# A selective-scan and mixture-of-experts layer: a third group of states multiplied by c on VectorE from PSUM

## The chip, the cores and the metric

The kernel runs on one core of a Trainium2 chip. The metric is the device time of one execution in microseconds (us); the median of several runs counts. The engines are TensorE (PE in the profile, its weight loads PEld), VectorE (DVE), ScalarE (ACT), GpSimd (POOL) and SyncE (SP, here only a queue for transfers).

## The reference

x holds 32 sequences of 256 steps and 128 features, fp32. Each sequence goes through a selective scan with residual, and then through a feed-forward network with 8 routed experts (the 2 best are used) and shared ones. Cut to what matters:

```python
u, o = split(layernorm(x) @ W_in.T)                  # 256 channels each
u = silu(conv4(u) + conv_b)
g = u @ W_gate.T                                     # 64 delta_lo, 16 b, 16 c
delta = softplus(g[..., :64] @ W_delta.T + delta_bias)
def step(h, inp):                                    # h: 256 channels x 16 states
    d_t, u_t, b_t, c_t = inp
    h = exp(A * d_t[..., None]) * h + (d_t * u_t)[..., None] * b_t[:, None, :]
    return h, einsum('nhs,ns->nh', h, c_t)           # y_t
y = (scan(step) + D * u) * sigmoid(o) * o
x = x + y @ W_out.T
x = x + ffn(layernorm(x))    # sum over experts of combine * (silu(x wg) * (x wu)) wd, + the shared one
```

## The kernel before

The program is a software pipeline written out by hand. Each engine has one list of instructions, in order; semaphores tie them together, and nothing reorders them later. Step k of the loop works on several sequences at once: layernorm, convolution and projections of sequences k+2 and k+3, delta of k+1, the scans of k, the output projection and router of k-1, and the feed-forward part of f = k-2.

The 256 channels x 16 states of a sequence are cut into 8 groups q = 0 to 7 of 128 partitions x 4 blocks x 256 steps (groups 0 to 3 are channel half 0, 4 to 7 half 1). For each group:

- ScalarE writes the decays exp(A d) into decay_ps, a PSUM tile with two halves; group q uses half q % 2 (decays, L489).
- GpSimd makes inject = (d u) b (inject_group, L410). dd holds d and d u, and SyncE spreads it to the tile rep by 8 transfers a sequence.
- VectorE scans (scan, L687). The result goes to the SBUF tile state, or, for the groups in OWN, back over its decays in decay_ps.
- The states are multiplied by c: GpSimd does it from state into read (read_group, L420), or, for the groups in OWN, VectorE from decay_ps into the single tile read_own (read_own_group, L699), and then it clears the first column of that half with a memset (L701).
- TensorE sums the products over the states into y_ps (sum_states, L894), which take_y (L722) multiplies by the gate.

Before a half of decay_ps is written again its last group must have been scanned, or, for a group of OWN, multiplied:

```python
if (q - 2) % GROUPS in OWN:
    act.wait_ge(decay_zero, owned_before(at - 1) + 1)
else:
    act.wait_ge(state_done, count(at - 1))
```

The feed-forward part has 7 pairs of chunks: gates (L902) and ups (L911) on TensorE, silu (L476) on ScalarE, gated_up (L708, called by pairs) on VectorE. Spread_comb (L923) spreads the combine weights over partitions, weigh (L716) multiplies by them, and down (L936) adds the 14 chunks into down_ps. Three PSUM banks, work0 to work2, are shared by all of this, by the table COMB_BANK and its like, so that many of these wait for one another. Softplus (L553) writes delta, which L790 on VectorE multiplies by u into dd; x1 (L781) is the sum of the projection and x; L804 and L809 are mean and variance of x_in, L816 and L827 those of x1.

Of the kernel before, what the change touches and what calls it, by code (L numbers as in the profile page):

```python
# [12 lines left out]
P = 128  # L13
# [32 lines left out]
OWN = (0, 4)  # L46
# [41 lines left out]
def build(nc, x, W_in, conv_w, conv_b, W_gate, W_delta, delta_bias, A_log, Dskip, W_out,  # L88
          gate_w, w_gate, w_up, w_down, sw_gate, sw_up, sw_down, out):
    with ExitStack() as ctx:  # L90
# [280 lines left out]
        def _(pool):  # L371
# [27 lines left out]
            def body(k, on):  # L399
# [48 lines left out]
                reads(6)  # L448
# [5 lines left out]
        def _(act):  # L454
# [14 lines left out]
            def body(k, on):  # L469
# [61 lines left out]
                if on(1) and not on(0):  # L531
                    act.wait_ge(ffn_loaded, 16 * len(ffn_loads))
                    act.wait_ge(padded, 2)
                    act.copy(ffn_gate[0][:], gate_staged).then_inc(ffn_high, 1)
                    act.copy(ffn_up[0][:], up_staged).then_inc(ffn_high, 1)
# [4 lines left out]
                if on(2):  # L540
                    n = k + 2
                    act.wait_ge(xnT_rest, n + 1)
                    act.copy(xnT_parts[1][:, TAPS - 1:], xnT_ps).then_inc(xnT_low, 1)  # L543
# [40 lines left out]
                if on(0):  # L584
                    decays(k, 5)
                if on(3) or on(-1):
# [6 lines left out]
                    act.activation(log_var[:], mean_var[:, :, 1], ACT.Ln, bias=eps[:, 0:1]).then_inc(ln_small, 1)  # L593
                    act.activation(neg_mean[:], mean_var[:, :, 0], ACT.Copy, scale=-1.0).then_inc(ln_small, 1)
# [34 lines left out]
        def _(dve):  # L629
# [44 lines left out]
            def body(k, on):  # L674
# [66 lines left out]
                if on(-2):  # L741
                    dve.wait_ge(best_done, TILES * (f + 1))
                    dve.wait_ge(h_done, PAIRS * f + EARLY)
                    for j in range(TILES):
                        dve.match_replace(out=marked_ps[:, j, :], in_to_replace=best[:, j, :], in_values=shifted[:, j, :],
                                          imm_value=1.0).then_inc(marked_done, 1)
                    dve.wait_ge(marked_done, TILES * (f + 1))
                    dve.wait_ge(expd_done, 2 * f + 1)
                    dve.scalar_tensor_tensor(out=picked, in0=marked_ps[:, :, FILL:], scalar=1.0, in1=expd[:],
                                             op0=ALU.is_equal, op1=ALU.mult).then_inc(comb_steps, 1)  # L750
                    dve.wait_ge(comb_steps, 4 * f + 1)
# [12 lines left out]
                if on(-3):  # L764
                    n = k - 3
                    dve.wait_ge(down_mm, CHUNKS * (n + 1))
                    dve.wait_ge(stored[n % 2], 16 * (n // 2))
                    dve.tensor_tensor(result[n % 2][:].rearrange("p j d -> p (j d)"), down_ps,  # L768
                                      x1[n % 2][:].rearrange("p j d -> p (j d)"), ALU.add).then_inc(result_done, 1)
                if on(-2):  # L770
# [6 lines left out]
                if on(-1):  # L777
                    n = k - 1
                    dve.wait_ge(proj_mm, n + 1)
                    dve.wait_ge(result_done, count(k - 2))  # L780
                    dve.tensor_tensor(x1[n % 2][:].rearrange("p j d -> p (j d)"), proj_ps,  # L781
                                      x_in[n % RX][:].rearrange("p j d -> p (j d)"), ALU.add).then_inc(x1_done, 1)
                if on(0):
                    scan(4)
                if on(1):
                    n = k + 1
                    dve.wait_ge(delta_done, n + 1)
                    for half in range(HALVES):
                        dve.wait_ge(rep_in[half], 16 * JB * n)
                    dve.tensor_tensor(dd[:, :, 1, :], delta_ps, u[n % RU][:], ALU.mult).then_inc(du_done, 1)  # L790
                if on(1) and not on(0):
                    dve.wait_ge(ffn_high, PARTS)
                    dve.tensor_tensor(ffn_gate[1][:], gate_staged, ffn_gate[0][:].bitcast(F32),
                                      ALU.subtract).then_inc(ffn_ready, 1)
                    dve.tensor_tensor(ffn_up[1][:], up_staged, ffn_up[0][:].bitcast(F32),
                                      ALU.subtract).then_inc(ffn_ready, 1)
                if on(0):
                    take_y(k, 0)
                if on(3):
# [5 lines left out]
                    last.then_inc(stats_done, 1)  # L805
                    dve.wait_ge(stats_done, n + 1 + count(k - 1))
# [3 lines left out]
                pairs(4)  # L810
# [7 lines left out]
                if on(0):  # L818
                    read_own_group(4)
                pairs(5)  # L820
                pairs(6)
                if on(-1):
# [3 lines left out]
                    for j in range(TILES):  # L826
                        dve.bn_aggr(mean_var[:, TILES + j, :], stats2[:, j, :]).then_inc(ln2_var, 1)  # L827
                if on(-2):
                    weigh(0)
                    weigh(1)  # L830
                if on(0):
                    scan(5)
                if on(-2):
                    weigh(2)
                    weigh(3)
                if on(0):
                    scan(6)
                    scan(7)
                if on(-2):
                    weigh(4)  # L840
# [7 lines left out]
                if on(-2):  # L848
                    weigh(5)
# [9 lines left out]
        def _(pe):  # L859
# [18 lines left out]
            def body(k, on):  # L878
# [90 lines left out]
                if on(-3):  # L969
                    pe.wait_ge(y_taken, HALVES * min(k, SEQS))  # L970
                    for chunk in (11, 12, 13):
                        down(chunk, f - 1)
                if on(-1):
# [11 lines left out]
                if on(2):  # L985
                    n = k + 2
                    if on(1):
                        pe.wait_ge(gate_done, k + 2)
                    pe.wait_ge(ln1_done, n + 1)
                    for j in range(TILES):  # L990
                        last = pe.matmul(xnT_ps[:, j * P:(j + 1) * P], xn[:, j, :], ident[:], start=(j == 0), stop=False,
                                         skip_group_check=True)
                    last.then_inc(xnT_mm, 1)
                if on(-2):
                    pe.wait_ge(comb_split, 2 * f + 2)
                    for j in range(TILES):
                        last = pe.transpose(combT_ps[:, j * P:(j + 1) * P], comb_parts[:, j, :].bitcast(F32), ident[:])  # L997
                    last.then_inc(combT_mm, 1)
                if on(0):
                    pe.wait_ge(result_done, count(k - 2))  # L1000
                    pe.wait_ge(y_taken, HALVES * k)
                    sum_states(k, 0)
                if on(2):
                    n = k + 2
# [4 lines left out]
                if on(0):  # L1009
                    sum_states(k, 1)  # L1010
                if on(2):
                    n = k + 2
# [8 lines left out]
                if on(0):  # L1021
                    sum_states(k, 2)
# [6 lines left out]
                if on(0):  # L1029
                    sum_states(k, 3)  # L1030
# [28 lines left out]
                if on(0):  # L1059
                    pe.wait_ge(y_taken, HALVES * k + 1)  # L1060
                    sum_states(k, 4)
                if on(-2):
# [4 lines left out]
                    if not on(0):  # L1067
                        pe.wait_ge(y_taken, HALVES * SEQS)
                        pe.wait_ge(result_done, f)
                    down(0, f)  # L1070
                    down(1, f)
# [13 lines left out]
                if on(-2):  # L1085
                    down(3, f)
                    down(4, f)
                    down(5, f)
# [11 lines left out]
                if on(-2):  # L1100
                    down(6, f)
                    down(7, f)
                    down(8, f)
# [5 lines left out]
                if on(-2):  # L1109
                    down(9, f)  # L1110
                    pe.wait_ge(hc_done, COMBS * f + 3)
                    spread_comb(4)
                if on(-1):
# [7 lines left out]
                if on(-2):  # L1121
                    pe.wait_ge(hc_done, COMBS * f + 4)
                    spread_comb(5)
                if on(0):
                    sum_states(k, 5)
                    sum_states(k, 6)
                if on(-2):
                    down(10, f)
                if on(-1):
# [19 lines left out]
                    ups(0, n)  # L1149

# [24 lines left out]
```

## Time and profile before

| | |
|---|---|
| median of 3 runs | 1239.75 us (1237.29 to 1242.07) |
| the profiled execution | 1238.7 us, its span 1237.0 us |
| mean granted TensorE clock | 0.966 of full speed |
| instructions | 25691 |
| busy: PE, DVE, ACT, POOL | 1123.3, 1066.9, 1011.0, 1067.5 us |

The busy times overlap. The page also has a row of the granted clock, where 9 stands for 90% or more of full speed. A wait is shown with the instruction that waited and the one that released it. The start of an instruction plus its length can reach over the start of the next one, since ends overlap; the time that an instruction takes from its engine's queue is the distance of the starts.

### The profile page before, as it was taken

To read this page: it belongs to the slowest core of one execution; us is meant where nothing else is said; L and a number is where in the kernel's file an instruction comes from. 1 tells how busy PE (TensorE), PEld (TensorE's weight loads), DVE (VectorE), ACT (ScalarE), POOL (GpSimd) and SP (SyncE) were. 2 spreads that over 40 slices of the span, in tenths; PEclk is the share of its full clock that TensorE was granted. 3 is DMA by queue.
4 is the path that set the end of the run, shared out by engine and by line. 5 is a ranking of instruction groups with operands and counts; after the bars stand their busy time and mean duration, and the time that the engine had idled before them with its cause. 6 is when DMAs were issued, how large, how long until landed. Compare 5 with 4: busy or idle time off the path is not lost. (4 is left out here: it accounts for less than half of the span.)

```text
span 1237.0 us, 25691 instructions
## 1 busy us (share of the span) xinstructions
PE 1123.3 (91%) x9075; PEld 919.1 (74%) x9075; DVE 1066.9 (86%) x1700; ACT 1011.0 (82%) x2119; POOL 1067.5 (86%) x502
## 2 busy tenths in 40 slices
PE   3456999999999999999999999999999999998887
PEld 2334778878778787887787878877878788876676
DVE  3277899999999999999998999999999999999854
ACT  2778888888888888888988888889888988897642
POOL 3299899999999999999998999999999999999810
PEclk8767999999999999999999999999999999999899
DMA  4444433344434333444343334443433344434000
GB/s 119 109 111 105 102 84 85 107 109 109 99 92 112 87 82 101 109 109 113 79 113 86 82 101 109 108 112 80 113 94 83 93 109 110 107 79 103 5 6 9
DMA packets 71482, 115.05 MB, mean 93 GB/s; under 512 B 8174, under 2 KB 30395, under 8 KB 71355
## 3 DMA queue, kind: packets, MB, share of 16 engines
q1 hardware_dynamic: 67178, 110.71, 35.0%
q10 hardware_dynamic: 4176, 2.70, 0.8%
q8 instruction: 72, 1.18, 0.4%
q14 instruction: 56, 0.45, 0.1%
HBM read 41.04 MB, written 5.24 MB: 37 GB/s over the span
## 5 line engine op out<-in xcount | busy, mean ns | idle before, releaser
L410 POOL TENSOR_TENSOR inject<-rep,bc 128x1024 f32<-128x1024 f32 x256 | 604.6, 2384 | 20.2 <-DMA rep<-dd 20.2
L420 POOL TENSOR_TENSOR read<-state,bc 128x1024 f32<-128x1024 f32 x192 | 452.2, 2376 | 10.2 <-DVE state L687 8.8
L687 DVE TENSOR_TENSOR_SCAN state<-decay_ps,inject 128x1024 f32<-128x1024 f32 x192 | 432.0, 2279 | 13.8 <-ACT decay_ps L489 13.0
L489 ACT ACTIVATE decay_ps<-rep,neg_a 128x255 f32<-128x255 f32 x1024 | 427.0, 465 | 8.9 <-DVE state L687 3.5
L936 PE MATMUL acc_ps<-ffn_down,features 128*128 128x128 f32 (+1 forms) x1792 | 244.8, 281 | 0.5 <-DVE features L716 0.5
L936 PEld LDWEIGHTS acc_ps<-ffn_down,features 128*128 128x128 f32 (+1 forms) x1792 | 220.3, 192 | 23.4 <-DVE features L716 7.4
L902 PE MATMUL work_ps<-xn2T_part,ffn_gate 128*128 128x256 f32 x1344 | 219.4, 300 | 6.7 <-ACT g_silu L476 3.0
L476 ACT ACTIVATE g_silu<-work_ps 128x512 f32<-128x512 f32 x224 | 134.9, 602 | 105.4 <-PE work_ps L902 94.8
L902 PEld LDWEIGHTS work_ps<-xn2T_part,ffn_gate 128*128 128x128 f32 x1344 | 180.0, 193 | 52.1 <-ACT g_silu L476 22.7
L911 PE MATMUL work_ps<-xn2T_part,ffn_up 128*128 128x256 f32 x1344 | 193.2, 284 | 0.0
L708 DVE TENSOR_TENSOR features<-g_silu,work_ps 128x512 f32<-128x512 f32 x224 | 149.8, 682 | 47.8 <-PE work_ps L911 47.4
L911 PEld LDWEIGHTS work_ps<-xn2T_part,ffn_up 128*128 128x128 f32 x1344 | 174.0, 191 | 0.5
L687 DVE TENSOR_TENSOR_SCAN decay_ps<-decay_ps,inject 128x1024 f32<-128x1024 f32 x64 | 146.3, 2286 | 8.2 <-POOL inject L410 8.2
L894 PE MATMUL acc_ps<-read,sum_sel 128*32 128x256 f32 x1536 | 125.8, 404 | 29.3 <-POOL read L420 25.5
L716 DVE TENSOR_TENSOR features<-features,work_ps 128x512 f32<-128x512 f32 (+1 forms) x192 | 116.3, 632 | 22.6 <-PE work_ps L923 21.9
L1017 PEld LDWEIGHTS work_ps<-xnT_part,wconv 128*128 128x128 f32 x768 | 100.5, 203 | 28.9 <-ACT xnT_part L543 27.7
L1017 PE MATMUL work_ps<-xnT_part,wconv 128*128 128x256 f32 x768 | 107.2, 299 | 13.2 <-ACT xnT_part L543 13.2
L444 POOL TENSOR_TENSOR shift<-neg_mean,rstd 128x4 f32<-128x4 f32 x36 | 7.3, 202 | 101.5 <-ACT rstd L596 101.5
L894 PEld LDWEIGHTS acc_ps<-read,sum_sel 128*32 128x32 f32 x1536 | 30.9, 109 | 69.9 <-POOL read L420 53.4
L699 DVE TENSOR_TENSOR read_own<-decay_ps,bc 128x1024 f32<-128x1024 f32 x64 | 77.5, 1211 | 0.1
L923 PE MATMUL work_ps<-combT,csel 40*128 40x256 f32 x352 | 75.9, 315 | 1.3 <-DVE features L708 1.2
L923 PEld LDWEIGHTS work_ps<-combT,csel 40*128 40x128 f32 x352 | 49.2, 185 | 22.9 <-issue 12.4
(130 smaller groups left out, 1250.5 us busy)
## 6 DMA issues: line engine op xcount, KB each, us to landing
rep<-dd SPq DMA_DIRECT2D x256, 256.0 KB, 4.7
bc<-bc_rows SPq DMA_DIRECT2D x64, 512.0 KB, 4.6
x_in<-in_L_attn_x_dram SPq DMA_DIRECT2D x32, 128.0 KB, 2.1
out_dram<-result SPq DMA_DIRECT2D x32, 128.0 KB, 1.8
bc_rows<-g_sb SPq DMA_DIRECT2D x32, 32.0 KB
state<-in_L_ffn_w_gate_dram ACTq DMA_DIRECT2D x1, 704.0 KB, 4.4
read<-in_L_ffn_w_up_dram ACTq DMA_DIRECT2D x1, 704.0 KB, 5.9
ffn_down<-in_L_ffn_w_down_dram ACTq DMA_DIRECT2D x1, 704.0 KB, 7.2
```

The costliest lines, as they stand in the source:

```text
L410: pool.tensor_tensor(inject[:, at % RI], du_all, b_all, ALU.mult).then_inc(inject_done, 1)
L420: pool.tensor_tensor(read[:, at % RR], state[:, at % RS], c_all, ALU.mult).then_inc(read_done, 1)
L476: act.activation(g_silu[p % 2][:], banks[GATE_BANK[p]][:], ACT.Silu).then_inc(silu_done, 1)
L489: last = act.activation(decay_ps[:, at % 2, j, 1:T], rep[(HALVES * n + half) % RP][:, j, 0, 1:T], ACT.Exp, scale=neg_a[:, col:col + 1])
L687: dve.tensor_tensor_scan(to, decays, inject[:, at % RI].rearrange("p j t -> p (j t)"), 0.0, ALU.mult, ALU.add).then_inc(state_done, 1)
L708: dve.tensor_tensor(features[:, 2 * p:2 * p + 2, :].rearrange("p c t -> p (c t)"), g_silu[p % 2][:], banks[UP_BANK[p]][:], ALU.mult).then_ ...
L894: last = pe.matmul(y_ps[j * CB:(j + 1) * CB, :], sum_sel[:], products[:, j, :], start=False, stop=(g == SG - 1), skip_group_check=True)
L902: last = pe.matmul(banks[GATE_BANK[p]][:, side * T:(side + 1) * T], ffn_gate[w][:, chunk * P:(chunk + 1) * P], xn2T_parts[n % 2][d][:], st ...
L911: last = pe.matmul(banks[UP_BANK[p]][:, side * T:(side + 1) * T], ffn_up[w][:, chunk * P:(chunk + 1) * P], xn2T_parts[n % 2][d][:], start= ...
L923: last = pe.matmul(banks[COMB_BANK[i]][:, at * T:(at + 1) * T], csel[:, (chunk - NSH) * P:(chunk - NSH + 1) * P], combT[:], start=True, st ...
L936: last = pe.matmul(down_ps[:, j * DIM:(j + 1) * DIM], features[0:r, chunk, j * P:(j + 1) * P], ffn_down[0:r, chunk, :], start=fresh and j ...
L1017: last = pe.matmul(conv_ps[:, half * T:(half + 1) * T], wconv[w][:, half, tap, :], xnT_parts[d][:, tap:tap + T], start=(w + d + tap == 0), ...
```

## The change

Group 6 joins the groups whose states stay in PSUM: VectorE multiplies them by c, and GpSimd no longer does. The four engines' lists are reordered with it. The groups left to GpSimd go from 6 to 5 a sequence.

```diff
-OWN = (0, 4)
+OWN = (0, 4, 6)
...
                 reads(5)
-                reads(6)
                 reads(7)
...
                     silu(0)
                     silu(1)
+                    silu(2)
...
-                    silu(2)
                     silu(3)
+                if on(1) and not on(0):
+                    act.wait_ge(ffn_loaded, 16 * len(ffn_loads))
+                    act.wait_ge(padded, 2)
+                    act.copy(ffn_gate[0][:], gate_staged).then_inc(ffn_high, 1)
+                    act.copy(ffn_up[0][:], up_staged).then_inc(ffn_high, 1)
...
+                if on(-2):
+                    act.wait_ge(combT_mm, f + 1)
+                    act.wait_ge(cb_mm, COMBS * f)
+                    act.copy(combT[:], combT_ps).then_inc(combT_done, 1)
...
                     act.activation(log_var[:], mean_var[:, :, 1], ACT.Ln, bias=eps[:, 0:1]).then_inc(ln_small, 1)
+                if on(0):
+                    decays(k, 5)
+                if on(3) or on(-1):
...
+                if on(0):
+                    pe.wait_ge(result_done, count(k - 2))
+                    pe.wait_ge(y_taken, HALVES * k)
+                    sum_states(k, 0)
...
                 if on(0):
+                    sum_states(k, 1)
+                    sum_states(k, 2)
                     sum_states(k, 3)
...
                     pe.wait_ge(hc_done, COMBS * f + 1)
                     spread_comb(2)
-                    pe.wait_ge(hc_done, COMBS * f + 2)
-                    spread_comb(3)
-                    down(2, f)
+                if on(0):
+                    pe.wait_ge(y_taken, HALVES * k + 1)
+                    sum_states(k, 4)
...
                 if on(0):
                     sum_states(k, 5)
+                if on(-2):
+                    down(8, f)
+                if on(0):
                     sum_states(k, 6)
                 if on(-2):
-                    down(10, f)
+                    down(9, f)
...
                     ups(0, n)
+                if on(-2):
+                    down(10, f)
```

The pieces stand in the order GpSimd (reads), ScalarE (silu to decays), TensorE (sum_states to down). On TensorE the output projection and the transposes of the combine weights also move behind sum_states(0), and the downs from 2 on move later. The moves on VectorE are shown by its order. The first place is the middle of a step on VectorE, around dd; the rows are of before, and then of the changed kernel (L789 and L802 are the statistics of x_in there, L795 is x1, L808 is dd, L814 and L823 are the statistics of x1).

```order
L687 SCALAR_TENSOR_TENSOR state<-decay_ps,inject 128x1024 x2
L781 TENSOR_TENSOR x_0<-work_ps,x_in 128x256
L687 SCALAR_TENSOR_TENSOR decay_ps<-decay_ps,inject 128x1024
L790 TENSOR_TENSOR dd<-work_ps,u 128x2x256
L722 TENSOR_TENSOR y_gated<-acc_ps,gate 128x256
L804 BN_STATS stats<-x_in 128x6 x2
L809 BN_AGGR mean_var<-stats 128x2 x2
L708 TENSOR_TENSOR features<-g_silu,work_ps 128x512
L816 BN_STATS stats<-x_0 128x6 x2
```

The same place on VectorE in the changed kernel:

```order
L687 SCALAR_TENSOR_TENSOR state<-decay_ps,inject 128x1024 x2
L789 BN_STATS stats<-x_in 128x6 x2
L795 TENSOR_TENSOR x_1<-work_ps,x_in 128x256
L802 BN_AGGR mean_var<-stats 128x2 x2
L808 TENSOR_TENSOR dd<-work_ps,u 128x2x256
L814 BN_STATS stats<-x_1 128x6 x2
L687 SCALAR_TENSOR_TENSOR decay_ps<-decay_ps,inject 128x1024
L823 BN_AGGR mean_var<-stats 128x2 x2
L708 TENSOR_TENSOR features<-g_silu,work_ps 128x512
L722 TENSOR_TENSOR y_gated<-acc_ps,gate 128x256
```

Scan 4 (the L687 into decay_ps) moved from ahead of dd to behind it, the statistics of x_in from behind dd to ahead of it, and the first take_y (L722) behind gated_up(4).

The second place is the end of a step on VectorE, from weigh(0) on, in the kernel before:

```order
L716 TENSOR_TENSOR features<-features,work_ps 128x256
L716 TENSOR_TENSOR features<-features,work_ps 128x512
L687 SCALAR_TENSOR_TENSOR state<-decay_ps,inject 128x1024
L716 TENSOR_TENSOR features<-features,work_ps 128x512 x2
L687 SCALAR_TENSOR_TENSOR state<-decay_ps,inject 128x1024 x2
L716 TENSOR_TENSOR features<-features,work_ps 128x512
L844 TENSOR_REDUCE top<-work_ps 128x2
```

The same place on VectorE in the changed kernel:

```order
L716 TENSOR_TENSOR features<-features,work_ps 128x256
L716 TENSOR_TENSOR features<-features,work_ps 128x512 x2
L687 SCALAR_TENSOR_TENSOR state<-decay_ps,inject 128x1024
L687 SCALAR_TENSOR_TENSOR decay_ps<-decay_ps,inject 128x1024
L716 TENSOR_TENSOR features<-features,work_ps 128x512
L699 TENSOR_TENSOR read_own<-decay_ps,bc 128x1024
L701 MEMSET decay_ps 128x4
L687 SCALAR_TENSOR_TENSOR state<-decay_ps,inject 128x1024
L845 TENSOR_REDUCE top<-work_ps 128x2
```

Scans 5 and 6 now follow each other, scan 6 writes decay_ps, and its product with c and the memset stand ahead of scan 7.

## Rows read from the trace of the kernel before

**Rows 1.** The page, parts 1 and 2: busy time by engine; clock in 40 slices.

```profile
PE 1123.3 (91%) x9075; PEld 919.1 (74%) x9075; DVE 1066.9 (86%) x1700; ACT 1011.0 (82%) x2119; POOL 1067.5 (86%) x502
...
PEclk8767999999999999999999999999999999999899
```

**Rows 2.** Busy time and clock in three stretches (PE, PEld, DVE, ACT, POOL).

```profile
72.00:108.00 36.00, 19.91 (x143) 12.42 (x143) 23.71 (x23) 26.42 (x55) 36.00 (x18) 0.76 0.39 95
605.00:640.00 35.00, 33.95 (x284) 27.96 (x283) 32.78 (x53) 30.61 (x66) 32.97 (x16) 1.00 0.40 99
640.00:675.00 35.00, 33.59 (x270) 27.68 (x270) 31.20 (x50) 29.02 (x64) 31.17 (x15) 0.95 0.34 91
```

**Rows 3.** Waits of VectorE, 220 to 605 us: total, times, longest.

```profile
DVE features L708 <- PE work_ps L911: 7.9, 13, 0.7
DVE features L716 <- PE work_ps L923: 4.7, 10, 0.5
DVE y_gated L722 <- PE acc_ps L894: 3.3, 11, 0.3
DVE state L687 <- ACT decay_ps L489: 2.5, 10, 0.3
```

**Rows 4.** Waits of GpSimd, 220 to 605 us.

```profile
POOL shift L444 <- ACT rstd L596: 14.4, 11, 1.3
POOL inject L410 <- DMA rep<-dd: 7.0, 11, 1.3
```

**Rows 5.** Groups by shape: count, then busy us, mean ns, idle before.

```profile
L420 POOL TENSOR_TENSOR read<-state,bc 128x1024 f32<-128x1024 f32 x192 | 452.2, 2376 | 10.2 <-DVE state L687 8.8
L687 DVE TENSOR_TENSOR_SCAN state<-decay_ps,inject 128x1024 f32<-128x1024 f32 x192 | 432.0, 2279 | 13.8 <-ACT decay_ps L489 13.0 <-POOL inject L410 0.8
...
L687 DVE TENSOR_TENSOR_SCAN decay_ps<-decay_ps,inject 128x1024 f32<-128x1024 f32 x64 | 146.3, 2286 | 8.2 <-POOL inject L410 8.2
```

**Rows 6.** Timeline of VectorE, 610 to 669 us: start, length, instruction.

```profile
610.35 4.47 DVE L687 TENSOR_TENSOR_SCAN state<-decay_ps,inject 128x1024 f32<-128x1024 f32 x2
...
618.55 0.67 DVE L708 TENSOR_TENSOR features<-g_silu,work_ps 128x512 f32<-128x512 f32 x1
...
631.50 0.40 DVE L781 TENSOR_TENSOR x<-work_ps,x_in 128x256 f32<-128x256 f32 x1
...
634.02 0.68 DVE L790 TENSOR_TENSOR dd<-work_ps,u 128x512 f32<-128x512 f32 x1
...
635.33 0.47 DVE L804 BATCH_NORM_STATS2 stats<-x_in 128x6 f32<-128x128 f32 x2
635.84 0.25 DVE L809 BATCH_NORM_AGGREGATE mean_var<-stats 128x2 f32<-128x6 f32 x2
636.78 0.69 DVE L708 TENSOR_TENSOR features<-g_silu,work_ps 128x512 f32<-128x512 f32 x1 [0.69 <-PE work_ps L911]
...
637.77 1.21 DVE L699 TENSOR_TENSOR read_own<-decay_ps,bc 128x1024 f32<-128x1024 f32 x1
...
639.13 1.34 DVE L708 TENSOR_TENSOR features<-g_silu,work_ps 128x512 f32<-128x512 f32 x2
...
645.41 4.47 DVE L687 TENSOR_TENSOR_SCAN state<-decay_ps,inject 128x1024 f32<-128x1024 f32 x2
...
668.42 0.40 DVE L781 TENSOR_TENSOR x<-work_ps,x_in 128x256 f32<-128x256 f32 x1
```

**Rows 7.** Timeline of ScalarE, 613 to 634 us.

```profile
613.06 3.46 ACT L489 ACTIVATE decay_ps<-rep,neg_a 128x255 f32<-128x255 f32 x8
...
632.50 0.60 ACT L553 ACTIVATE work_ps<-z_sb 128x512 f32<-128x512 f32 x1
```

**Rows 8.** Timeline of TensorE, 619 to 651 us.

```profile
619.40 0.87 PE L902 MATMUL work_ps<-xn2T_part,ffn_gate 128*128 128x256 f32 x6
...
650.82 0.73 PE L894 MATMUL acc_ps<-read,sum_sel 128*32 128x256 f32 x8 [0.40 <-POOL read L420]
```

More of the change, by code:

```diff
@@ L530, in body @@
                     decays(k, 3)
[L531 to L535, printed above, removed]
+                if on(2):
+                    n = k + 2
+                    act.wait_ge(xnT_rest, n + 1)
+                    act.copy(xnT_parts[1][:, TAPS - 1:], xnT_ps).then_inc(xnT_low, 1)
                 if on(-2):
@@ L776, in body @@
                     scan(3)
[L777 to L798, printed above, removed]
                 if on(3):
@@ L809, in body @@
                         dve.bn_aggr(mean_var[:, j, :], stats1[:, j, :]).then_inc(ln1_var, 1)
-                pairs(4)
+                if on(1):
+                    n = k + 1
+                    dve.wait_ge(delta_done, n + 1)
+                    for half in range(HALVES):
+                        dve.wait_ge(rep_in[half], 16 * JB * n)
+                    dve.tensor_tensor(dd[:, :, 1, :], delta_ps, u[n % RU][:], ALU.mult).then_inc(du_done, 1)
                 if on(-1):
@@ L818, in body @@
                 if on(0):
-                    read_own_group(4)
-                pairs(5)
-                pairs(6)
+                    scan(4)
                 if on(-1):
@@ L827, in body @@
                         dve.bn_aggr(mean_var[:, TILES + j, :], stats2[:, j, :]).then_inc(ln2_var, 1)
+                pairs(4)
+                if on(0):
+                    take_y(k, 0)
+                    read_own_group(4)
+                pairs(5)
+                pairs(6)
                 if on(-2):
@@ L830, in body @@
                     weigh(1)
+                    weigh(2)
                 if on(0):
                     scan(5)
+                    scan(6)
                 if on(-2):
-                    weigh(2)
                     weigh(3)
                 if on(0):
-                    scan(6)
+                    read_own_group(6)
                     scan(7)
-                if on(-2):
-                    weigh(4)
                 if on(-1):
@@ L848, in body @@
                 if on(-2):
+                    weigh(4)
                     weigh(5)
@@ L972, in body @@
                         down(chunk, f - 1)
+                if on(2):
+                    n = k + 2
+                    if on(1):
+                        pe.wait_ge(gate_done, k + 2)
+                    pe.wait_ge(ln1_done, n + 1)
+                    for j in range(TILES):
+                        last = pe.matmul(xnT_ps[:, j * P:(j + 1) * P], xn[:, j, :], ident[:], start=(j == 0), stop=False,
+                                         skip_group_check=True)
+                    last.then_inc(xnT_mm, 1)
+                if on(0):
[3 more added lines that the diff above has]
+                if on(-2):
+                    pe.wait_ge(comb_split, 2 * f + 2)
+                    for j in range(TILES):
+                        last = pe.transpose(combT_ps[:, j * P:(j + 1) * P], comb_parts[:, j, :].bitcast(F32), ident[:])
+                    last.then_inc(combT_mm, 1)
                 if on(-1):
@@ L986, in body @@
                     n = k + 2
[L987 to L1004, printed above, removed]
                     pe.wait_ge(xnT_high, n + 1)
@@ L1109, in body @@
                 if on(-2):
-                    down(9, f)
+                    down(7, f)
                     pe.wait_ge(hc_done, COMBS * f + 3)
                     spread_comb(4)
+                    pe.wait_ge(hc_done, COMBS * f + 4)
+                    spread_comb(5)
                 if on(-1):
```

66 lines of the change are left out of this document (32 added, 34 removed).

## The prediction

> **What bounds the kernel now.** I read the page's busy shares first. TensorE shows 91%, VectorE and GpSimd 86% each, and the granted clock stands at 9 tenths or more in nearly every slice after the first ramp [rows 1]. No engine is plainly alone in front, so the next view is busy time by stretch. In 35 us of the steady state TensorE is busy 33.95, GpSimd 32.97, VectorE 32.78 and ScalarE 30.61, at clock 1.00 [rows 2]. From one sum x1 (631.50) to the next (668.42) a sequence once took 36.92 us, and there the clock fell, 0.95 in its window [rows 2, 6]. The usual period is shorter, as the next but one view shows.
>
> Third view: who waits. In 385 us (11 periods) GpSimd waits about 1.3 us a period for ScalarE's rstd and 0.6 for the DMA of rep [rows 4]. VectorE waits 1.7 a period in four places: about 0.7 for the ups before gated_up(4), 0.45 for the spread of the combine weights, 0.3 for y, 0.25 for the decays [rows 3]. So every engine has small holes and none runs without them. What bounds is a ring through several engines, and the question for the change is how long the ring is with the new orders. The reader should take the ring from the timeline: scan 7 of one sequence ends at 610.35 + 4.47 = 614.82 and of the next at 645.41 + 4.47 = 649.88, so the period is 35.06 [rows 6].
>
> **The change part by part.** *Removed:* one GpSimd product a sequence, 2.376 us [rows 5], 32 times. GpSimd's busy time falls from 33.0 in 35 us [rows 2] to 30.6. That time alone shortens nothing beyond the holes around it.
>
> *Added on VectorE:* one read_own product of 1.21 us and the memset behind it. In the timeline the pair takes 637.77 to 639.13, so 1.36 us [rows 6]. Scan 6 writes PSUM instead of SBUF: a scan takes 2.286 us into PSUM and 2.279 into SBUF [rows 5], so I cost that at nothing. A VectorE that never waited would need 35.06 − 1.71 + 1.36 = 34.7 us. This is the floor of the new period.
>
> The Trainium skill (Perfetto Trace Analysis, Identifying the Most-Contended Engine) ranks VectorE and GpSimd by occupancy and says to relieve the highest. By that rule the change makes the highest higher, from 1067 us to about 1107 with 32 pairs. At an unchanged 86% share, that would give 1283 us, an estimate from the page's ranking; the trace's idle time, 1.7 us a period, says that part of it can be absorbed.
>
> *The ring, first leg, from the end of scan 7 to the end of softplus.* ScalarE cannot write decays of group 1 of the next sequence before scan 7 has read that half of decay_ps. It does the two groups in 613.06 to 616.52, then loads a table, then silu 0; TensorE and ScalarE go on in turn until softplus ends at 632.50 + 0.60 = 633.10 [rows 7]. That is 18.28 after scan 7. The new orders leave this leg nearly as it is. Gates(2) started at 619.40 [rows 8], while pair 0, for which it must wait, was ready at 618.55 + 0.67 = 619.22 [rows 6]; TensorE comes to it earlier now, since down(10) and the sums move off, so I take 0.14 off: 18.14. Moving sum_states(0) ahead of combT makes TensorE wait for the result on VectorE, some 0.7 us, but conv still waits for ScalarE's xnT_part as before, so that is hidden; if that cover were gone it would cost up to 0.7.
>
> *Second leg, from dd to the end of scan 7, on VectorE.* Before, scan 4 stood ahead of dd, and so VectorE came to dd only at 634.02, 0.92 after softplus. The new order has dd ahead of scan 4. VectorE would be there at 631.36 (its x1 time, 0.14 earlier) + 0.40 + 0.47 + 0.25, some 632.5, while softplus ends at 632.96: it waits half a microsecond. Scan 4 (2.52 between 631.50 and 634.02, less 0.32 for the x1 handover: 2.20) now lies behind dd, in this leg. The old leg is 649.88 − 634.02 = 15.86, of which 0.30 + 0.69 + 0.47 = 1.46 were waits: 14.40 of work. New work: 14.40 + 2.20 (scan 4) + 1.36 (read_own 6) − 0.73 (the statistics of x_in, 0.47 and 0.25, which now stand ahead of dd) = 17.23 [rows 6].
>
> Waits left in it: gated_up(4) began 3.68 after softplus ended (636.78 − 633.10) because of silu 4, gates 5 and ups 4, which still follow softplus; VectorE arrives 3.5 after dd's start, so 0.14. Pair 6 keeps about 0.1. Weigh(1) needs spread_comb(1), which needs pair 6: VectorE has only weigh(0) to cover it, since the mean of x1 is aggregated earlier now. I take 0.3, next to the 0.45 seen there before [rows 3]; bounds 0 and 0.7. The sum is 17.23 + 0.54 = 17.77.
>
> Ring: 18.14 + 0.04 (softplus to dd) + 17.77 = 35.9, against 35.06: **0.85 us longer**. With every wait in the second leg gone it is 35.4; with the old 1.46 of waits kept, 36.85. What is late next is scan 5, then decays 7 and the logits, but each of these has over 1 us of room. GpSimd's product 7 waits for scan 7, about 2 us, as product 6 no longer fills that time. Inject 1 behind it is ready long before scan 1, so this costs nothing in the steady state. SyncE's eight rep transfers leave after ScalarE's copy of dd, which keeps its place behind silu 4: no change. The read_own tile is single: read_own(6) waits for the sum of group 4, and read_own(0) for that of group 6; both sums are over 1 us ahead.
>
> *Ends.* All parts run together for 27 sequences: 27 × 0.85 = +23. In the first two sequences with scans GpSimd is busy 36.00 of 36.00 us [rows 2], so there a removed product counts. At most 2 × 2.38 comes off; I take 2 × 1.8, as product 7 must wait for scans 6 and 7 with read_own between. The casts of the FFN weights on ScalarE now stand ahead of xnT's high part and no longer cover its round trip over TensorE, +0.9. The last three sequences: +1 (0 to 4). Sum against the profiled execution's own 1238.7 us: 1238.7 + 23 + 1 − 3.6 + 0.9 = 1260. The median of the runs is 1.0 above that execution, well inside the doubt.
>
> **The rivals.** *A, the ring grows (forecast):* 1260. Its own range is 1246 (ring 35.4) to 1275 (36.4). For it: a chain in which each link is a semaphore or an engine's order. Against it: errors of 0.1 us in a link, times some ten links.
>
> *B, TensorE's clock falls as well.* In the period with 36.92 TensorE had waited only 0.40 us, at 650.82 for product 6 [rows 8], before the clock fell to half, and the period lost 1.86. The new orders give TensorE about 0.8 us more idle a period, with holes of 0.6 to 0.7 before the first sum and before spread_comb(1). If a third of the periods fall, 9 × 1.86 = +17: 1277; all of them, +50: 1310. Against it: the two waits of 0.4 that each period has around xnT never did it. The Trainium skill (TensorE: Matmul & The Clock Gate, A second HAM failure mode: psum-queue depth-cycling) says that short idles between groups of matmuls, often repeated, make the clock swing. This trace shows that twice in the steady state, so the rule speaks for B.
>
> *C, faster: VectorE's new order closes its holes.* Then the period is VectorE's floor, 34.7 plus at most 0.2, and the time 1238.7 − 0.36 × 27 − 2.7, some 1226, or 1232 with the 0.2. For it: take_y now stands behind gated_up(4), so two holes are offered other work, and GpSimd no longer holds TensorE at the sum of group 6. Against it: softplus. The ring must be at least 0.9 shorter than I sum it, which decides it: that takes softplus within 17.3 of scan 7 or no wait at all after dd and 0.4 less.
>
> *D, no change:* the ring is 35.1 to 35.2 and the ramp's gain pays for it, 1234 to 1245. For it: half of what C needs.
>
> **Chances.** A 0.50, B 0.17, C 0.17, D 0.16. Below 1230 only the best of C is left (0.12), above 1285 the worse half of B (0.07): the range is 1230 to 1285. About 0.5%, or 6 us, is what a measurement of this kernel tells from no change. C gives faster 0.17; D gives same 0.16; A and B give slower 0.67.
>
> **What would show it.** The distance of two x1 sums in the middle of the trace: 35.9 if I am right, 34.9 or less for C. A VectorE wait for softplus before dd of about 0.5 a period, and almost none on POOL anywhere. GpSimd waiting near 2 us a period for scan 7. Granted clock below 1.00 in steady windows would mean B. I am wrong if the leg from scan 7 to softplus is a microsecond shorter, that is, if TensorE's queue, relieved of its waits for GpSimd, lets gates and ups run ahead of what I took as fixed.

## The result, and the profile after the change

The changed kernel takes 1268.8 us (median of 4 runs, 1267.7 to 1269.4), the kernel before 1239.6 on the same chip (1237.3 to 1242.1). The ratio is 1.023, with a 95% interval of 1.021 to 1.026: slower by 2.3%. The profiled execution took 1269.4 us, with a span of 1267.4 against 1237.0 before, so 30.4 us of span are to be explained.

The page of the changed kernel, its busy times, its clock by slices and its chain that ended last (share of the span by engine):

```profile
PE 1136.1 (90%) x9075; PEld 931.0 (73%) x9075; DVE 1106.2 (87%) x1764; ACT 1015.0 (80%) x2119; POOL 996.2 (79%) x470
...
PEclk9767999999999999999999999999999999998898
...
PE 70%; ACT 16%; issue 5%; DVE 4%; POOL 4%; ACTq 1%; SPq 0%; DMA 0%; DVEq 0%; POOLq 0%
```

Against [rows 1], GpSimd has 71 us less, VectorE 39 us more, and the clock is as it was. The third line had no counterpart before, since the page of before follows its chain for 1% of the span only. It is the line to stop at. The change put work on VectorE, VectorE is busier than it was, and yet the chain that ended last lies on VectorE for only 4% of the span.

Two stretches of the steady state (columns as in [rows 2]):

```profile
605.00:640.00 35.00, 33.94 (x283) 28.04 (x281) 33.31 (x52) 29.75 (x64) 29.79 (x15) 1.00 0.40 100
640.00:675.00 35.00, 33.37 (x276) 27.41 (x276) 33.17 (x50) 29.76 (x63) 29.80 (x15) 1.00 0.38 100
```

The clock is 1.00 in both, where the second stretch of [rows 2] has 0.95. GpSimd fell from 32.97 busy to 29.79. Its waits, and VectorE's, from 220 to 605 us, answering to [rows 3, 4]:

```profile
DVE dd L808 <- ACT work_ps L552: 6.8, 10, 0.7
DVE features L716 <- PE work_ps L925: 2.9, 11, 0.3
DVE features L708 <- PE work_ps L913: 2.4, 10, 0.2
DVE state L687 <- ACT decay_ps L488: 2.3, 10, 0.3
...
POOL read L420 <- DVE state L687: 34.4, 21, 3.1
```

VectorE's waits of 0.7 for the ups and 0.45 for the spread have become 0.24 and 0.26, and a new wait of 0.68 for softplus stands ahead of dd. GpSimd waits about 3 us a period for the scans. One period of VectorE (start, length, instruction):

```profile
611.48 0.69 DVE L808 TENSOR_TENSOR dd<-work_ps,u 128x512 f32<-128x512 f32 x1 [0.68 <-ACT work_ps L552]
...
619.42 1.28 DVE L716 TENSOR_TENSOR features<-features,work_ps 128x512 f32<-128x512 f32 x2 [0.26 <-PE work_ps L925]
...
625.59 1.21 DVE L699 TENSOR_TENSOR read_own<-decay_ps,bc 128x1024 f32<-128x1024 f32 x1
626.88 0.06 DVE L701 MEMSET decay_ps<- 128x4 f32 x1
626.95 2.29 DVE L687 TENSOR_TENSOR_SCAN state<-decay_ps,inject 128x1024 f32<-128x1024 f32 x1
...
647.52 0.69 DVE L808 TENSOR_TENSOR dd<-work_ps,u 128x512 f32<-128x512 f32 x1 [0.68 <-ACT work_ps L552]
```

From dd to dd is 36.04, the new period; [rows 6] gives 35.06. Scan 7 ends at 629.24, 17.76 after dd began. That is the second leg, forecast as 17.77. Now the chain that ended last, in the same period. Each line is a start, a length and what the chain lay on; it leaves TensorE only where it must:

```profile
613.41 0.98 PE work_ps L904 x6
...
616.67 1.44 PE work_ps L913 x12
...
618.14 0.70 DVE features L708
618.84 0.04 issue
618.88 0.83 PE work_ps L925 x4
...
636.86 0.72 PE work_ps L965 x6
...
637.60 0.60 ACT gate L517
...
643.71 3.12 PE work_ps L1015 x24
...
648.80 0.61 ACT g_silu L475
```

Read it as a loop with two parts. The **first part** runs from gates(5) to the gate projection (L965, L963 before) and lies in TensorE's queue, but for one gated_up (618.14) that the queue waits for. The **second part** runs from the gate projection through ScalarE's gate, table load, decays and casts, the conv and silu(4), back to gates(5). TensorE's timeline gives both parts in every kernel. Before:

```profile
600.00 0.98 PE L902 MATMUL work_ps<-xn2T_part,ffn_gate 128*128 128x256 f32 x6
...
622.29 0.87 PE L963 MATMUL work_ps<-xnT_part,wo 128*128 128x256 f32 x6
...
635.06 0.97 PE L902 MATMUL work_ps<-xn2T_part,ffn_gate 128*128 128x256 f32 x6
```

That is 22.29 and 12.77. After, in the changed kernel:

```profile
613.41 0.98 PE L904 MATMUL work_ps<-xn2T_part,ffn_gate 128*128 128x256 f32 x6
...
618.88 0.83 PE L925 MATMUL work_ps<-combT,csel 40*128 40x256 f32 x4 [0.47 <-DVE features L708]
...
636.70 0.86 PE L965 MATMUL work_ps<-xnT_part,wo 128*128 128x256 f32 x6
...
649.45 0.98 PE L904 MATMUL work_ps<-xn2T_part,ffn_gate 128*128 128x256 f32 x6
```

That is 23.29 and 12.75. So the whole difference of 0.98 a period lies in the first part, and TensorE has one wait in it, 0.47 ahead of spread_comb(1), which it did not have before.

### The profile page after: what moved, and what is told of

It is laid out like the page before. It is cut to its first block, busy times and chain, and to the rows that moved or that the text cites. A ratio compares the mean times of both kernels' runs of the same rounds, so it can differ in the third digit from the quotient of the medians.

```text
span 1267.4 us, 25723 instructions
## 1 busy us (share of the span) xinstructions
PE 1136.1 (90%) x9075; PEld 931.0 (73%) x9075; DVE 1106.2 (87%) x1764; ACT 1015.0 (80%) x2119; POOL 996.2 (79%) x470
## 4 chain that ended last, share of the span: by engine, by line
PE 70%; ACT 16%; issue 5%; DVE 4%; POOL 4%; ACTq 1%; SPq 0%; DMA 0%; DVEq 0%; POOLq 0%
PE work_ps L904 14%; PE acc_ps L938 13%; PE work_ps L913 11%; PE acc_ps L896 8%; PE work_ps L1015 7%; ACT decay_ps L488 7%; PE work_ps L925 5%; ACT L520 3%; PE work_ps L1072 2%; PE work_ps L1042 2%; POOL inject L410 2%; PE work_ps L1115 2%; DVE features L708 2%; PE work_ps L965 2%; POOL read L420 2%
## 5 line engine op out<-in xcount | busy, mean ns | idle before, releaser
L420 POOL TENSOR_TENSOR read<-state,bc 128x1024 f32<-128x1024 f32 x160 | 379.7, 2382 | 108.8 <-DVE state L687 107.7
L687 DVE TENSOR_TENSOR_SCAN state<-decay_ps,inject 128x1024 f32<-128x1024 f32 x160 | 362.4, 2282 | 15.0 <-ACT decay_ps L488 14.0
L938 PEld LDWEIGHTS acc_ps<-ffn_down,features 128*128 128x128 f32 (+1 forms) x1792 | 222.9, 194 | 27.8 <-issue 25.0
L687 DVE TENSOR_TENSOR_SCAN decay_ps<-decay_ps,inject 128x1024 f32<-128x1024 f32 x96 | 218.8, 2279 | 11.7 <-POOL inject L410 11.7
L708 DVE TENSOR_TENSOR features<-g_silu,work_ps 128x512 f32<-128x512 f32 x224 | 150.2, 682 | 34.7 <-PE work_ps L913 33.4
L699 DVE TENSOR_TENSOR read_own<-decay_ps,bc 128x1024 f32<-128x1024 f32 x96 | 116.5, 1214 | 0.1
L896 PE MATMUL acc_ps<-read,sum_sel 128*32 128x256 f32 x1280 | 98.4, 402 | 14.7 <-POOL read L420 14.6
L896 PE MATMUL acc_ps<-read_own,sum_sel 128*32 128x256 f32 x768 | 63.4, 403 | 0.4 <-DVE read_own L699 0.4
```

What stands on the lines that cost most here:

```text
L420: pool.tensor_tensor(read[:, at % RR], state[:, at % RS], c_all, ALU.mult).then_inc(read_done, 1)
L687: dve.tensor_tensor_scan(to, decays, inject[:, at % RI].rearrange("p j t -> p (j t)"), 0.0, ALU.mult, ALU.add).then_inc(state_done, 1)
L708: dve.tensor_tensor(features[:, 2 * p:2 * p + 2, :].rearrange("p c t -> p (c t)"), g_silu[p % 2][:], banks[UP_BANK[p]][:], ALU.mult).then_ ...
L896: last = pe.matmul(y_ps[j * CB:(j + 1) * CB, :], sum_sel[:], products[:, j, :], start=False, stop=(g == SG - 1), skip_group_check=True)
L938: last = pe.matmul(down_ps[:, j * DIM:(j + 1) * DIM], features[0:r, chunk, j * P:(j + 1) * P], ffn_down[0:r, chunk, :], start=fresh and j ...
```

## The experiments

Each was timed against the kernel before on its own chip (medians 1240.5 to 1242.3), and each ratio has its 95% interval.

**1. The new orders without the product.** Group 6 is read by GpSimd again.

```diff
-OWN = (0, 4, 6)
+OWN = (0, 4)
 reads(5)
+reads(6)
 reads(7)
-read_own_group(6)
 scan(7)
```

> The changed kernel's lists, but group 6 goes back to GpSimd. Ring theory: the leg from dd to scan 7 loses the product and its memset, 1.36 us, and the ring is 18.24 + 0.04 + 16.39 = 34.7 us a period, unless another ring (GpSimd: 33 us of work and its two waits) holds it near 35.0; 1230 to 1240 us, at or below the kernel before. Rival 1, the new orders are what costs: near 1268 still. Rival 2, VectorE's added work alone costs and the orders do nothing: 1239 to 1241, with a period of 35.05.

Measured: 1263.0 us, ratio 1.017 (1.013 to 1.020), period 35.94. Without the product the second leg on VectorE is 16.37 us (dd at 610.33 to the end of scan 7 at 626.70), 1.39 shorter than in the changed kernel, and the period gives back 0.10. The ring as the prediction summed it, which expected 34.7 here, does not explain that. TensorE's queue has the same hole as in the changed kernel:

```profile
612.26 0.97 PE L904 MATMUL work_ps<-xn2T_part,ffn_gate 128*128 128x256 f32 x6
...
617.72 0.82 PE L925 MATMUL work_ps<-combT,csel 40*128 40x256 f32 x4 [0.47 <-DVE features L709]
...
635.44 0.86 PE L965 MATMUL work_ps<-xnT_part,wo 128*128 128x256 f32 x6
```

The first part is 23.18, 0.89 over before, and the new orders alone make it.

**2. The product without the new orders.**

```diff
-OWN = (0, 4)
+OWN = (0, 4, 6)
 reads(5)
-reads(6)
 reads(7)
 scan(6)
+read_own_group(6)
 scan(7)
```

> The lists of the kernel before, with only group 6 given to VectorE (its product and memset stand between scan 6 and scan 7). Ring theory: the product lies in the leg from dd to scan 7, whose waits come from TensorE behind softplus and dd and cannot take it up, so the period is 36.2 to 36.4 and the time 1268 to 1280. Rival 1, the new orders are what costs: 1240. Rival 2, VectorE has 1.7 us of waits a period to absorb it: the period stays below 35.5 and the time below 1255.

Measured: 1313.5 us, ratio 1.056 (1.052 to 1.061), period 37.55, where the ring theory expected 36.2 to 36.4. TensorE waits for weigh(4), which stands behind the product and scan 7 on VectorE, and then the clock falls (the second fence: windows, with the busy times of PE, PEld, DVE, ACT, POOL and the granted clock):

```profile
608.30 1.12 PE L936 MATMUL acc_ps<-ffn_down,features 128*128 128x128 f32 x4 [1.17 <-DVE features L715]
609.07 1.63 PE L902 MATMUL work_ps<-xn2T_part,ffn_gate 128*128 128x256 f32 x6
610.50 1.48 PE L911 MATMUL work_ps<-xn2T_part,ffn_up 128*128 128x256 f32 x6
611.78 0.91 PE L902 MATMUL work_ps<-xn2T_part,ffn_gate 128*128 128x256 f32 x6
```

```profile
606.00:608.50 2.50, 1.33 (x19) 0.62 (x18) 2.46 (x5) 1.93 (x5) 0.76 (x1) 0.99 0.00 0
608.50:612.00 3.50, 3.50 (x18) 3.50 (x18) 2.98 (x5) 2.75 (x5) 3.50 (x2) 0.52 0.10 16
```

Gates(0) and ups(0) take 2.71 (609.07 to 611.78) where they took 1.50. So the new orders are not idle: with the product in place they are worth 1.5 us a period.

**3 and 4. A pad on VectorE**, two bn_stats into an unused tile (0.47 us together): ahead of x1 in run 3, behind dd in run 4 (the edit shown is that of run 4).

```diff
+for j in range(TILES):
+    dve.bn_stats(spare[:, j, :], u[k % RU][:, 0, j * P:(j + 1) * P])
 scan(4)
```

> The changed kernel with two more bn_stats on VectorE (about 0.4 us a period, result unused) between scan 3 and x1, ahead of dd. Ring theory: VectorE waits 0.68 us for softplus there, so the period stays 36.04 and the time within 4 us of the changed kernel's 1268.8. Rival, VectorE is simply full: +0.4 us a period, 1280 to 1283. (If x1, which TensorE waits for, counts: part of it.)

> The same two bn_stats, but behind dd, ahead of scan 4. Ring theory: they lie in the ring, save for the 0.24 us that gated_up(4) waits: +0.15 to +0.4 us a period, 1273 to 1282. Rival, VectorE is simply full: 1280 to 1283, the same as with the pad ahead of dd.

Measured: 1268.5 (1.021, 1.018 to 1.025) and 1264.6 (1.017, 1.013 to 1.021); periods 36.01 and 36.00. Ahead of dd the pad eats the wait for softplus (0.29 is left of 0.68), as expected. Behind dd it should have lengthened the ring, and does not: the wait of 0.24 ahead of gated_up(4) is gone from VectorE's waits, and the rest went into a small gap there. So that piece of the leg follows TensorE's ups(4). Run 4's 4 us less come mostly from its first two periods (35.71 and 35.99; in the changed kernel 37.26 and 36.93); the cause of that stays open.

**5. sum_states(4) back ahead of the spreads**, in the changed kernel; **6. the same piece moved behind spread_comb(1)**, in the kernel before; **7.** run 5 with down(10) ahead of gates(0) and sums 5 and 6 side by side as well.

```diff
 ups(6, f)
+sum_states(k, 4)
 spread_comb(0)
 spread_comb(1)
 spread_comb(2)
-sum_states(k, 4)
```

> The changed kernel with one piece of TensorE's queue put back: sum_states(4) stands again between ups(6) and spread_comb(0), ahead of the spreads. Theory 1, TensorE's queue from gates(5) to the gate projection (23.29 us in the changed kernel, 22.29 before) and ScalarE's work from there back to gates(5) (12.75 and 12.77) set the period: the 1.1 us of sums cover the 0.47 us that TensorE now waits ahead of spread_comb(1), the stretch falls to about 22.8 and the period from 36.04 to 35.5; 1250 to 1256 us. Theory 2, VectorE's leg from dd to scan 7 (17.75) and ScalarE's first leg (18.24) set it: VectorE's queue is untouched, the period stays at 36.0 and the time at 1265 to 1271.

> The kernel before with the same piece moved the other way: sum_states(4) stands behind spread_comb(1). VectorE, ScalarE and GpSimd keep the lists of before. Theory 1: TensorE waits ahead of spread_comb(1) for the product of pair 6, 0.3 to 0.6 us per sequence, which nothing makes up; period 35.06 to 35.4 or 35.6, 1249 to 1258 us. Theory 2: the period stays at 35.06 and the time within 3 us of before.

> The changed kernel with sum_states(4) ahead of the spreads as in the run above, and besides with down(10) back ahead of gates(0) and sum_states(5) and (6) side by side. Theory 1: fewer changes between small pieces in TensorE's queue take another 0.1 to 0.4 us off the stretch; period 35.1 to 35.4, 1238 to 1251 us. Theory 2: 36.0, 1265 to 1271.

Measured: 1279.4 (1.030, 1.026 to 1.034), period 36.49; 1256.7 (1.013, 1.008 to 1.017), period 35.74; and 1280.0 (1.030, 1.026 to 1.034), period 36.49. From the side of before theory 1 holds, with a period 0.14 above its range. The other three engines' lists are untouched, TensorE gets the hole of 0.47, and the first part is 22.98 (607.53 to 630.51):

```profile
607.53 0.98 PE L902 MATMUL work_ps<-xn2T_part,ffn_gate 128*128 128x256 f32 x6
...
612.99 0.50 PE L923 MATMUL work_ps<-combT,csel 40*128 40x256 f32 x2 [0.47 <-DVE features L708]
...
630.51 0.86 PE L963 MATMUL work_ps<-xnT_part,wo 128*128 128x256 f32 x6
```

From the side of after both theories missed: the hole is gone, other waits have come (the table below), and the period is 0.45 longer, 36.49 where theory 1 had 35.5 and theory 2 had 36.0. Run 7 is no better. In run 5 the spreads start later, so VectorE comes to weigh(0) only at 625.78, 6.04 after gates(5); in the changed kernel it is 5.33 (618.74). The whole run of scans and the product shifts with it, and TensorE waits at its end (chain of run 5):

```profile
632.45 1.13 DVE read_own L699
...
633.72 2.29 DVE state L687
...
636.20 0.69 DVE features L716
636.89 0.14 issue
637.03 0.94 PE work_ps L904 x6
```

So there is a second chain through VectorE, nearly as long as TensorE's queue, and this piece of the new order serves it.

**8. The whole of TensorE's old list** under the changed lists of the others.

> The changed kernel with the whole of TensorE's list as it is before the change; the lists of VectorE, ScalarE and GpSimd stay as changed, and group 6 stays in PSUM. Theory 1: if the other engines follow without a wait, TensorE's stretch is 22.3 again and the period 35.0 to 35.4 (1238 to 1250 us); what is over that is a wait that the other engines' new lists bring (the spread of pair 2 on VectorE stands earlier than TensorE's spread of it). Theory 2: 36.0, or longer by such waits; 1265 or more.

Measured: 1315.1 (1.059, 1.055 to 1.063), period 37.22, and 38.5 in seven of 27. One down waits 1.33 us for a weigh, a later one 0.53. In the periods of 38.5 the clock is 0.55 in the 3 us after that (613 to 616); in the others it stays at 1.00. The run does not decide between the theories: the period is far above theory 1's 35.4, with waits for VectorE's new list of the kind that it named, and theory 2 allowed for such waits too. A list fits the lists beside it or it does not; one alone cannot be taken back.

**10. Run 7 with weigh(4) ahead of scan 7; 11. run 2 with weigh(4) ahead of scan 7.**

```diff
 read_own_group(6)
+weigh(4)
 scan(7)
-weigh(4)
```

> The changed kernel with sum_states(4) first, down(10) ahead of gates(0) and sums 5 and 6 together, as in the earlier run of 1280 us (period 36.49), and now weigh(4) ahead of scan 7 on VectorE. Theory 1 in its second form: in that run gates(0) waited 0.43 to 0.68 us for weigh(4), which stands behind product 6 and scan 7, so TensorE and VectorE form one chain there (gates(5), spread, weigh(0), scans 5 and 6, product 6, scan 7, weigh(4), gates(0)). With weigh(4) 2.3 us earlier this chain is loose, and TensorE's own queue sets the stretch: period 35.5 to 35.9, 1245 to 1260 us. The rival, that VectorE's whole run of 17.7 us from dd to the end of scan 7 binds: 36.4 to 36.5, 1277 to 1283.

> The kernel before with product 6 alone (1313.5 us, period 37.55) and weigh(4) moved ahead of scan 7 on VectorE; nothing else. Theory 1, second form: product 6 costs only because weigh(4), and behind it gates(0), stand after it, where the kernel before has 1.1 us of slack; with weigh(4) ahead of scan 7 the wait of 1.2 us and the fall of the clock once a period go: clock back from 0.95 to 0.96 or more, period 35.1 to 35.7, 1240 to 1262 us. The rival, that VectorE's added 1.28 us of work binds wherever it stands: 36.3 or more, 1275 to 1314 us.

Measured: 1294.1 (1.042, 1.037 to 1.048), period 37.04; and 1294.0 (1.042, 1.037 to 1.046), period 37.10. Run 11 did away with the fall of the clock, which is 1.00 from 602 to 650, and won 0.45 a period on run 2. Both times are far off the expectation of theory 1. In run 11 the rival's range (36.3 or more, 1275 to 1314) holds the result; in run 10 both missed. They show what ties scan 7 to TensorE (run 11):

```profile
638.48 2.28 DVE L686 TENSOR_TENSOR_SCAN state<-decay_ps,inject 128x1024 f32<-128x1024 f32 x1
...
640.80 1.67 ACT L488 ACTIVATE decay_ps<-rep,neg_a 128x255 f32<-128x255 f32 x4 [1.14 <-DVE state L686]
...
642.49 1.28 ACT L493 ACT_TABLE_LOAD   x1
643.78 1.09 ACT L475 ACTIVATE g_silu<-work_ps 128x512 f32<-128x512 f32 x2
644.43 0.77 PEld L912 LDWEIGHTS work_ps<-xn2T_part,ffn_up 128*128 128x128 f32 x6 [1.20 <-ACT g_silu L475]
```

ScalarE's last decays wait for scan 7 to free its half of decay_ps, behind them stand the table load and silu(0), and ups(1) waits for silu(0). Whatever stands ahead of scan 7 on VectorE delays ups(1) 3.7 us later. Moving weigh(4) there relieved gates(0) and burdened ups(0), which waits for weigh(5), and ups(1).

**9. A piece out of the first part, in the kernel before**: sum_states(k-1, 7) behind ups(3), a third gate buffer, take_y behind scan(1); on TensorE the transposes of xn also stand behind that sum, ahead of the last three downs and the output projection. **12.** The same with gated_up(1) ahead of the product of group 0, where run 9 showed the next wait, and sum_states(k, 0) behind the rest product of xn.

```diff
 ups(2, f)
-sum_states(k - 1, GROUPS - 1)
 gates(3, f)
 ...
 ups(3, f)
+sum_states(k - 1, GROUPS - 1)
```

> The kernel before with one piece moved out of TensorE's stretch from gates(5) to the gate projection: sum_states(k-1, 7), 0.57 us between ups(2) and gates(3), goes behind ups(3); the gate of y gets a third buffer, so that ScalarE's gate does not wait for take_y, and take_y(k-1, 1) stands behind scan(1) on VectorE. Total work of every engine is the same. Theory 1 (TensorE's stretch of 22.29 and ScalarE's 12.77 set the period): 21.7 plus 12.77, period 34.4 to 34.6, 1219 to 1230 us, faster than before. Theory 2 (VectorE's legs set it): take_y is later and nothing on VectorE is shorter, period 35.05 to 35.4, 1238 to 1252 us.

> The kernel of the run that moved sum_states(k-1, 7) behind ups(3) (period 35.08, same time as before), with two more moves: on VectorE gated_up(1) stands ahead of the product of group 0, and on TensorE sum_states(k, 0) stands behind the rest product of xn. What it tests: in that run gates(3) waited 0.28 us for gated_up(1), the end of an unbroken run of VectorE from weigh(0) on, and the conv's operand came 0.25 us later. If the period is the longest of several chains that lie within 0.3 us of one another (TensorE's queue; VectorE's run from weigh(0) to gated_up(1) and (2), then gates(3) and the gate projection), loosening the second lets the first gain show, up to where gated_up(2) binds: period 34.7 to 34.9, 1226 to 1237 us. If something else holds the period at 35.06, 1237 to 1245.

Measured: 1239.8 (0.999, 0.997 to 1.002), period 35.08; and 1253.2 (1.009, 1.007 to 1.011), period 35.34, but 37.4 to 37.7 in five of 27. Run 9 is as its theory 2 had it, and run 12 lies above both of its expectations. In run 9 the first part shrank by 0.24 (600.74 to 622.79), then gates(3) met gated_up(1); the second part grew by as much, with the conv later and a sum waiting 0.21 for GpSimd. The wait in run 9:

```profile
621.98 0.97 PE L902 MATMUL work_ps<-xn2T_part,ffn_gate 128*128 128x256 f32 x6 [0.28 <-DVE features L708]
```

In run 12 it was the gate projection that met gated_up(2):

```profile
631.44 0.97 PE L961 MATMUL work_ps<-xnT_part,wo 128*128 128x256 f32 x6 [0.58 <-DVE features L708]
```

In run 12 TensorE also waits about 0.4 for GpSimd ahead of gates(5), and its second part is 13.13. None of these versions beats the kernel before.

## Why the prediction was right in its sum, and where it was not

**The forecast and its number.** "The ring grows", 1260 us; measured 1268.8, slower, inside its range. The period was forecast as 35.9 and is 36.04; the first leg as 18.14 and is 18.24 (629.24 to 647.48); the second as 17.77 and is 17.76. Its rows after the change, scan 4 and the product behind dd and the statistics ahead of it, are as summed. (Its own terms, 18.14, 0.04 and 17.77, add up to 35.95, not 35.9.) That the sum came so close is in part luck: the same way of adding gave 34.7 for run 1, where 35.94 was measured. It fits here because in this kernel the way over VectorE and the way over TensorE's queue are nearly equally long.

**The step that failed is what those legs were taken to mean.** The prediction treated VectorE's legs as the one chain that sets the period, so that its +2.20 and +1.36 would be the cause. Run 1 takes the 1.36 out and gives back 0.10; run 4 puts 0.47 in, at a place where the leg has slack, and costs nothing. The loop passes from gates(5) to the gate projection by more than one way. Before and after the change two of these ways are within 0.3 us of one another. The table has the usual period of each kernel:

| kernel | first part | wait(s) of TensorE in it | second part |
|---|---|---|---|
| before | 22.29 | none | 12.77 |
| changed | 23.29 | 0.47 ahead of spread_comb(1) | 12.75 |
| 1, orders only | 23.18 | 0.47, the same | 12.76 |
| 6, before with sum 4 late | 22.98 | 0.47, the same | 12.75 |
| 5, sum 4 first | 23.74 | 0.28 spread_comb(2), 0.42 gates(0) | 12.75 |
| 2, product only | 24.81 | 1.17 down(10), then slower matmuls | 12.75 |
| 11, product, weigh(4) first | 24.35 | 0.75 ups(0), 0.98 ups(1) | 12.75 |
| 9, sum 7 late | 22.05 | 0.28 gates(3) | 13.02 |
| 12, and gated_up(1) first | 22.21 | 0.58 gate projection | 13.13 |

The way over TensorE's queue: its 1.0 us of growth is the hole of 0.47 and about 0.5 of the same matmuls taking longer to get through. Run 6 has the hole and 0.2 of that, from moving sum 4 alone. The distances of the starts say where the 0.53 of the changed kernel lies: gates 0.17, spreads 0.16, ups, the skip product and the transposes behind the delta projection 0.11 each, the delta projection 0.10, and off it 0.13 for the sums and 0.10 for the downs. These pieces have other neighbours than before; no run undoes them one by one, so that the neighbours are the cause is not shown. The way over VectorE: gates(5), spread, weigh(0), scans 5 and 6, product 6, scan 7, decays, table, silu(0), ups(1). In the changed kernel its end is:

```profile
632.25 0.60 ACT L475 ACTIVATE g_silu<-work_ps 128x512 f32<-128x512 f32 x1
632.99 0.90 PE L913 MATMUL work_ps<-xn2T_part,ffn_up 128*128 128x256 f32 x6
```

Silu(0) ends at 632.85 and ups(1) starts at 632.99, with TensorE back to back, so this way is at most 0.14 shorter. Before, the same distance was 0.25 (618.44 to 618.69). That is why one edit undone gives so little. The product costs 0.10 on top of the orders, the orders cost 0.88 on top of before without it and save 1.51 with it.

**The term seen from the wrong engine.** The prediction had the wait at the spread: "Weigh(1) needs spread_comb(1), which needs pair 6", 0.3 in VectorE's leg. VectorE's wait is 0.26. TensorE's for the same handover is 0.47, with 18 us of queue behind it. The prediction had this hole too, at 0.6 to 0.7, but only under rival B, where it asked whether the clock would fall; TensorE's queue was no term of the ring. The prediction also took 0.14 off the first leg, as "down(10) and the sums move off". The pieces that moved stayed in TensorE's queue ahead of the gate projection; the leg is 0.04 shorter.

**The ends, the term that was mis-sized.** The steady part came out right by two errors that cancel: the middle 27 periods together are 22.8 us longer, forecast +23. That is 27 x 0.98 = 26.5 where 27 x 0.85 was forecast, less 3.7 that before lost in its longer periods, which the forecast left out although it had seen the longest (half of the 3.7, [rows 6, 8]). The ends were forecast at -1.7 and are +7.7 (30.4 less 22.8, rounded). Until the first x1 +1.9, of which 0.8 is the FFN casts (forecast +0.9) and 0.9 the first conv, whose 24 matmuls took 5.29 us instead of 4.37; the cause of that stays open. The first two periods +1.1, where GpSimd's missing product was to give -3.6: busy without a pause [rows 2] did not make it the bound there. The last two periods and the tail +4.7, forecast +1: before, these ran 34.62 and 32.35, now 36.96 and 33.51, and the tail behind the last x1 is 1.2 longer; TensorE's longest wait there is 3.16 for x1, before it was 2.92 for a product of GpSimd. Why the drain lost more than it had to is open.

**The rivals.** B, the clock: did not come, it is 1.00 in the steady state, though the period has holes of 0.47 and 0.68. The Trainium skill (TensorE: Matmul & The Clock Gate, A second HAM failure mode: psum-queue depth-cycling) was taken to speak for B. In the changed kernel the trace does not follow it; in run 2 the clock does swing, with one longer wait of 1.17 a period. The prediction also read the swing twice in the steady state of before. The trace has it once there, at 651.4; the second, at 1126, stands behind the last of the 27 full periods, after a wait of 2.79. C, faster: needed what VectorE's floor of 34.7 would allow; the waits it counted on did go (1.71 a period in [rows 3] to about 1.4, half of it moved to softplus), and bought nothing, since other ways bind. The prediction's estimate from the ranking by occupancy gave 1283: VectorE's busy share is 87%, not 86, and it is 4% of the chain. D fell with the period.

## What to carry to other kernels

When several engines are 80 to 90% busy and none waits long, look for a loop that closes on itself and cut it at two instructions that stand in every variant: here the second part's median was 12.75 to 12.77 in twelve kernels, and nearly all that happened was in the first. Only in runs 9 and 12, which moved a piece into it, did it grow. Where two engines wait at the same handover, price the wait on the one with more work queued behind it, not on the one where the wait is shorter. And where orders are laid out together, undoing one piece tests the piece in the surroundings of the others: test it from the kernel before too (run 6), or its price may come out with the wrong sign (run 5).

## What the runs showed of the hardware

In run 2 the granted clock was 0.51 to 0.53, so 1.2 GHz nearly throughout, for 3.5 us in each of six periods, and was 1.00 in the stretches between them (537 to 570, 612 to 646). TensorE had been busy 1.33 of the 2.5 us ahead of it, with one wait of 1.17. Holes of 0.75 and 0.98 us, under 3 us apart, in run 11 left it at 1.00. In before it fell to 0.54 (651.4 to 654.9) behind a wait of only 0.40, and in run 12 to 0.59 (373.0 to 376.5) behind one of 0.54, in a period of 37.5 where most are 35.34. So in these runs the length of a single wait does not tell whether the clock falls. In both run 2 and run 8 it is still near 1 while TensorE waits (0.99 and 0.88) and low when gates(0) run: the stall costs its own length and then, in run 2, 1.2 us more in gates(0) and ups(0).
